# Attention two of a two-attention block: one set of scores, stacked through DRAM, subtracted and transposed

## What is computed

```python
qkv = flat @ w_qkv.T                       # 16 heads of 16 dimensions
# chunks of 64 tokens; k_cat, v_cat: the chunk before and the chunk itself (zeros before the first)
scores = jnp.einsum('bclhd,bcmhd->bchlm', q, k_cat) * scale
scores = jnp.where(valid[None, :, None, None, :], scores, jnp.finfo(scores.dtype).min)
attn = jax.nn.softmax(scores, axis=-1)
out = jnp.einsum('bchlm,bcmhd->bclhd', attn, v_cat)
out = out.reshape(B, T, H * HD) @ w_out.T
```

## Time and profile before

| | |
|---|---|
| median of 3 runs | 174.55 us (174.52 to 174.95) |
| the profiled execution | 174.46 us |
| its span in the trace | 172.6 us |
| PE, DVE, ACT, POOL busy | 92%, 72%, 59%, 51% of the span |
| chain that ended last | PE 82%, DVE 9% |

### The profile page before, as it was taken

One profiled execution on the slowest core, in us unless ns is written; L12 is line 12 of the kernel. 1 busy time (PEld: TensorE's weight loads), 2 busy tenths in 40 slices (PEclk: granted clock), 3 DMA queues, 4 the chain that ended last, 5 costly groups with the idle time before them and its releaser, 6 DMA issues.

```text
span 172.6 us, 4016 instructions
## 1 busy us (share of the span) xinstructions
PE 158.0 (92%) x1466; PEld 122.8 (71%) x1466; DVE 124.4 (72%) x330; ACT 101.2 (59%) x219; POOL 87.7 (51%) x132
## 2 busy tenths in 40 slices
PE   0879689999999999998999999999999999999872
PEld 0378669988897887986777747887678766575551
DVE  0496687866574684829998998978989779987220
ACT  3102867788685759877665837376483773353420
POOL 0814569564463538634873568425593276554000
PEclk9999999999999999999999999999999999999998
DMA  5639500000000000000000000000100001001001
GB/s 113 211 85 341 186 0 6 0 0 8 0 0 0 4 2 4 0 0 4 0 0 0 0 4 4 4 0 0 33 1 30 4 0 34 30 0 36 30 25 39
DMA packets 4979, 5.34 MB, mean 31 GB/s; under 512 B 440, under 2 KB 4920, under 8 KB 4960
## 3 DMA queue, kind: packets, MB, share of 16 engines
q1 hardware_dynamic: 4496, 4.80, 9.0%
q10 hardware_dynamic: 464, 0.28, 0.6%
HBM read 4.02 MB, written 1.06 MB: 29 GB/s over the span
## 4 chain that ended last, share of the span: by engine, by line
PE 82%; DVE 9%; issue 3%; ACT 2%; DMA 2%; POOL 1%; DVEq 0%
PE bank L549 15%; PE bank L513 9%; PE bank L537 7%; PE bank L493 7%; PE bank L528 5%; PE bank L605 5%; PE bank L596 5%; PE bank L642 4%; PE bank L546 4%; PE bank L502 3%; PE bank L432 3%; DMA X<-x 2%; PE bank L638 2%; PE bank L632 2%; PE bank L625 2%
## 5 line engine op out<-in xcount | busy, mean ns | idle before, releaser
L1070 ACT ACTIVATE PT<-bank 128x512 f32<-128x512 f32 x64 | 38.2, 599 | 31.4 <-PE bank L549 22.6
L330 POOL TENSOR_TENSOR Qk<-Qn,con 128x512 f32<-128x512 f32 x32 | 37.1, 1163 | 27.3 <-PE bank L549 26.9
L319 POOL TENSOR_SCALAR SB<-SB,NM 128x256 f32<-128x256 f32 x64 | 30.6, 491 | 20.6 <-DVE NM L869 20.4
L869 DVE CUSTOM_DVE_ANT_0 SB<-bank,Tk 128x256 f32<-128x256 f32 x64 | 24.3, 420 | 18.4 <-PE bank L513 18.4
L549 PE MATMUL bank<-Qk,Kf 128*128 128x512 f32 x64 | 32.6, 591 | 0.0
L881 DVE TENSOR_TENSOR D<-con,NM 128x512 fp32r<-128x512 f32 x32 | 28.9, 903 | 2.0 <-PE bank L549 1.9
L873 DVE TENSOR_REDUCE NM<-bank 128x4 f32<-128x512 f32 x32 | 21.9, 684 | 2.0 <-PE bank L528 1.8
L513 PE MATMUL bank<-KH,QM 128*128 128x256 f32 x64 | 18.9, 318 | 1.9 <-ACT QM L1052 1.9
L537 PE MATMUL bank<-con,SB 128*128 128x128 f32 x128 | 19.2, 272 | 0.0
L528 PE MATMUL bank<-Km,Qs 128*128 128x512 f32 x32 | 16.8, 524 | 0.0
L513 PE MATMUL bank<-KL,QM 128*128 128x256 f32 x64 | 16.5, 281 | 0.0
(11 more groups left out here) (129 smaller groups left out, 298.3 us busy)
## 6 DMA issues: line engine op xcount, KB each, us to landing
Tk<-bias_rows SPq DMA_DIRECT2D x4, 384.0 KB, 4.7
X<-x SPq DMA_DIRECT2D x4, 256.0 KB, 4.6
y<-Y SPq DMA_DIRECT2D x8, 128.0 KB, 1.7
Kf<-w_qkv SPq DMA_DIRECT2D x1, 768.0 KB, 7.7
Kf<-w_outb SPq DMA_DIRECT2D x1, 256.0 KB, 7.8
con<-consts ACTq DMA_DIRECT2D x1, 145.5 KB, 3.3
PT<-w_qk ACTq DMA_DIRECT2D x1, 128.0 KB, 4.6
PT<-buckets SPq DMA_DIRECT2D x1, 64.0 KB, 3.0
```

The costliest lines, as they stand in the source:

```text
L319: last = nc.gpsimd.tensor_scalar(rows_of, rows_of, -1.0, NM[:, i % 2, 2 * u + nt:2 * u + nt + 1], ALU.mult, ALU.add)
L330: nc.gpsimd.tensor_tensor(Qk[:, idx % QRING, :].rearrange("p (a v q) -> p v a q", a=4, v=2), Qn[:, b % 2, g, c * CHUNK:(c + 1) * CHUNK].un ...
L869: last = V.tensor_tensor_reduce(SB[:, idx % SRING, nt * CH:(nt + 1) * CH], half, Tk[:, u, nt * P:nt * P + CH], 1.0, LOWEST, ALU.add, ALU.m ...
L1070: A.activation(PT[:, u, :], bank[Z_BANK + u % 2][:], ACT.Exp, scale=-SCALE if is_a(i) else SCALE).then_inc(p_ready, 1)
```

## The change

In attention two the scores are computed once. ACT copies the projected queries from PSUM as fp32r (`QHL[:, 0]`), DVE subtracts that from the bank for the low part (`QHL[:, 1]`), and the same for keys (`KHL`). SP writes these to DRAM, per dimension as three terms: high, low, high for the queries; high, high, low for the keys. SP reads them back so that a head's 16 x 3 = 48 rows lie on consecutive partitions: two heads on partitions 0 to 47 and 64 to 111, the queries of each in its own half of the columns and zeros elsewhere (POOL's `zeros`, once). One fp32r matmul of 128 x 128 then gives two heads' scores with all three products summed; a block has four. DVE takes the maxima and subtracts them from the bank into `SB`; the PE transposes (`shifted_b`). The masks, `Km`, `Qs`, `Qk`, `Kf`, `D` and `minus`, go.

With it: XTl moves from DVE to POOL (`low_x`), the copies of the values from DVE to ACT (`value_rows`), `VB` has three buffers, the fills of `VB` move from before the loop to steps 8 to 10. The projections of attention two start three steps earlier, those of attention one and its `finish` shift by one or two.

```diff
-        XR_A, Q_A, K_A, V_A = -8, -6, -4, -2
-        XT_B, GM_B, GV_B, Q_B, K_B, V_B = -9, -8, -7, -4, -3, -2
-        FINISH = [(range(UNITS - 1), (10, 13), (12, 15), (13, 16), (15, 18)),
+        TIMES_A = [(range(1, 3), (-8, -6, -5, -4)), (range(3, BATCH), (-9, -7, -6, -5))]
+        XT_B, GM_B, GV_B, Q_B, K_B, V_B = -12, -11, -10, -7, -6, -5
+        FINISH = [(IN_A, (9, 12), (14, 14), (15, 15), (17, 17)),
+                  (range(BATCH, UNITS - 1), (10, 13), (12, 15), (13, 16), (15, 18)),
                   (range(UNITS - 1, UNITS), (10, 13), (12, 15), (13, 16), (14, 17))]
...
+            def put_terms(b, terms, hl, dup, ready, written):
+                sp.wait_ge(ready, BATCH + b + 1)
+                if dup == 0:
+                    sp.dma_start(terms[b, :, 0:2, :], hl[:].bitcast(F32)).then_inc(written, 16)
+                    sp.dma_start(terms[b, :, 2, :], hl[:, 0, :].bitcast(F32)).then_inc(written, 16)
...
+            def get_queries(b):
+                sp.wait_ge(q_written, 32 * (b + 1))
+                for j in range(4):
+                    for par in range(2):
+                        src = bass.AP(q_terms.tensor, (b * P + (2 * j + par) * HD) * TERMS * 2 * TOK,
+                                      [[2 * TOK, SLOT], [CHUNK, 2 * NCH], [1, CHUNK]])
+                        sp.dma_start(Q4[par * CHUNK:par * CHUNK + SLOT, b % 2, j, :, par, :].bitcast(F32), src).then_inc(q_loaded, 16)
+            def get_keys(b):
+                sp.wait_ge(k_written, 32 * (b + 1))
+                for par in range(2):
+                    src = bass.AP(k_terms.tensor, (b * P + par * HD) * TERMS * 2 * TOK,
+                                  [[2 * TOK, SLOT], [2 * HD * TERMS * 2 * TOK, 4], [1, 2 * TOK]])
+                    sp.dma_start(K4[par * CHUNK:par * CHUNK + SLOT, b % 2].rearrange("p j g n -> p j (g n)").bitcast(F32), src).then_inc(k_loaded, 16)
+            for b in range(BATCH + 2):
+                if b < BATCH:
+                    i = BATCH + b
+                    put_terms(b, q_terms, QHL, 0, q_ready, q_written)
+                    put_terms(b, k_terms, KHL, 1, k_ready, k_written)
+                    if b == 0:
+                        sp.wait_ge(zeroed, ZEROS)
+                    if b >= 2:
+                        sp.wait_ge(s_done, BLK * (i - 1))
+                    get_queries(b)
+                    get_keys(b)
+                if b >= 2:
+                    i = BATCH + b - 2
+                    for cp in range(2):
+                        n = halves(i - 1) + cp + 1
+                        sp.wait_ge(res_ready, n)
+                        sp.dma_start(out[i - BATCH, cp * P:(cp + 1) * P, :], Y[:, cp]).then_inc(y_out[cp], 16)
...
             def scores_b(i, u):
+                n = (i - BATCH) % 2
                 c, g = u // 2, u % 2
+                first, step = ((0, 0), (0, CHUNK), (2 * CHUNK, -CHUNK), (2 * CHUNK, CHUNK))[c]
+                for j in range(4):
+                    keys = K4[:, n, j, g, :]
+                    window = bass.AP(keys.tensor, keys.offset + first, [keys.ap[0], [step, 2], [1, CHUNK]])
+                    last = nc.tensor.matmul(bank[S_BANK + u % 2][:, j * P:(j + 1) * P], Q4[:, n, j, g * NCH + c].rearrange("p e n -> p (e n)"), window,
+                                            start=True, stop=True)
+                return last
...
                 if u == 0:
-                    pe.wait_ge(q_ready, i + 1)
                     if is_a(i):
                         pe.wait_ge(k_ready, i + 1)
-                if idx >= 2:
+                    else:
+                        pe.wait_ge(q_loaded, 128 * (i - BATCH + 1))
+                        pe.wait_ge(k_loaded, 32 * (i - BATCH + 1))
+                if idx >= BATCH * BLK + 2:
+                    pe.wait_ge(subb_ready, idx - BATCH * BLK - 1)
+                elif idx >= 2:
                     pe.wait_ge(max_ready, idx - 1)
...
-            def diagonal(i, u):
+            def below_max(i, u):
                 idx = i * BLK + u
-                n = 4
                 dve.wait_ge(max_ready, idx + 1)
-                dve.wait_ge(z_done, idx - DRING + 1)
+                dve.wait_ge(z_done, idx - SRING + 1)
+                V.tensor_tensor(SB[:, idx % SRING, :].rearrange("p (h m) -> p h m", h=4),
+                                bank[S_BANK + u % 2][:].rearrange("p (h m) -> p h m", h=4),
+                                NM[:, i % 2, 4 * u:4 * u + 4].unsqueeze(2).to_broadcast([P, 4, P]), op=ALU.subtract).then_inc(subb_ready, 1)
```

More of the change, by code:

```diff
@@ L117, in build @@
         WoutK = sb("WoutK", [P, TT, P])
-        WQh, WQl, WKh, WKl = (sb(n, [P, 2, P], F32R) for n in ("WQh", "WQl", "WKh", "WKl"))
+        WQK = sb("WQK", [P, 4, 2, P], F32R)
+        WQh, WQl, WKh, WKl = (WQK[:, n] for n in range(4))
         WTh = sb("WTh", [P, CT, 3 * CH], F32R)
@@ L255, in build @@
         AHEAD = 2
+        ZEROS = 12
         GROUPS = [(0, 1), (1, 2), (2, BATCH)]
@@ L416, in wait_bank_f @@
                 if i > 0:
[L417 to L420, removed]
+                    pe.wait_ge(k_ready, i)
             def project_a(i, step):
@@ L543, in shifted_b @@
                 z = bank[Z_BANK + u % 2]
[L544 to L550, removed]
+                below = SB[:, (i * BLK + u) % SRING, :]
+                for j in range(4):
+                    last = nc.tensor.transpose(z[:, j * P:(j + 1) * P], below[:, j * P:(j + 1) * P], ident)
+                return last
             def scores(i, u):
@@ L685, in _ @@
                     weights_b((4, 5, 7, 9).index(t))
-                for step, when in enumerate((XR_A, Q_A, K_A, V_A)):
-                    for i in due(t, when, IN_A[1:]):
-                        project_a(i, step)
+                for units, when in TIMES_A:
+                    for step in range(4):
+                        for i in due(t, when[step], units):
+                            project_a(i, step)
                 for step, when in enumerate((XT_B, GM_B, GV_B, Q_B, K_B, V_B)):
@@ L782, in queries_keys @@
                 else:
-                    b = i - BATCH
-                    if which == 0:
-                        dve.wait_ge(qh_ready, i + 1)
-                        if b >= 2:
-                            dve.wait_ge(s_done, BLK * (i - 1))
-                        for v in range(2):
-                            last = V.tensor_scalar(Qs[:, b % 2, :, :, v, :], Qn[:, b % 2].rearrange("p g (c q) -> p g c q", c=NCH),
-                                                   con[:, C_HALF + v:C_HALF + v + 1], None, ALU.mult)
-                        last.then_inc(q_ready, 1)
+                    f = bank[G_BANK if which == 0 else F_BANK]
+                    hl, ready, done = (QHL, qh_ready, q_ready) if which == 0 else (KHL, kh_ready, k_ready)
+                    dve.wait_ge(ready, i + 1)
+                    V.tensor_tensor(hl[:, 1, :], f[:], hl[:, 0, :].bitcast(F32), op=ALU.subtract).then_inc(done, 1)
             def low_weights(n):
@@ L1108, in _ @@
                     head_queries(ahead // BLK, ahead % BLK)
-                for step, when in enumerate((XR_A, Q_A, K_A)):
-                    for i in due(t, when, IN_A[1:]):
-                        projected(i, step)
+                for units, when in TIMES_A:
+                    for step in range(3):
+                        for i in due(t, when[step], units):
+                            projected(i, step)
                 for step, when in enumerate((GV_B + 1, Q_B, K_B)):
```

206 lines of the change are left out of this document (83 added, 123 removed).

## The result

| | before | after |
|---|---|---|
| median | 174.61 us (174.52 to 174.95) | 207.66 us (207.60 to 208.42) |
| ratio, 95% interval | | 1.191 (1.188 to 1.194) |
| span of the profiled execution | 172.6 us | 206.4 us |

What follows compares the result with a forecast made beforehand. TensorE's work was taken to bound the kernel. With waits for loads, units 4 to 7 start at 84.3, 105.5, 126.9 and 151.0; 27.5 more ends the span at 178.5, and 1.9 on top gives 180.4 us; range 171 to 189.

Runs made afterwards that it cites:

- e5: Changed kernel with all six projections of attention two one step earlier: 208.1 us.
- e7: Changed kernel with VectorE taking the low parts of attention two's queries and keys ahead of the same step's maximum: 204.9 us.
- e9: e7 with K's projection one step earlier, in the same step as Q's: 197.8 us.
- e10: Changed kernel with keys projected in the queries' step, low parts ahead of the maximum, output stores a round later, 30 transposes before each wait: 183.8 us.

## What to carry to other kernels

When a change puts a transfer between two engines on the critical path, price it as a round: last store ready, every issue at its own shape, landing at its own number of partitions; then multiply by how often it comes. If the sum shows waits of some microseconds on TensorE, add the slow clock behind each to the same sum; filling the wait with harmless matmuls gave back 8 of 192 us here. A store that waits for a fixed event in the same queue eats what you gain ahead of it, as it did in e5, e7 and e9. And before trusting a gain on the bounding engine, add up the second engine in the same step: a step of 0.86 us on one beside 1.38 on the other may not gain all that the first one saves.

## What the runs showed of the hardware

- A load of 384 KB to 48 partitions landed in 6.0 us, the same bytes to 128 partitions in 4.1 (medians, two such loads under way), with a DMA share of 1.02 and 0.97.
- Issuing a load with eight runs of 256 B on each of 48 partitions takes SP 0.62 us, with one run of 2 KB 0.42; now and then one takes 2 us.
- Four fp32r products of 128 x 128 x 128 with new weights take 0.40 us at full clock and 0.75 at half; the first four behind a wait 0.64 and 1.09.
- Behind PE waits of 5.9 to 11.1 us the mean clock over the next 7 to 8 us of unbroken matmuls was 0.62 to 0.72. With transposes in the first 3.3 us of waits of 3.3 to 4.4 us it stayed at 1.00 (e10).
